# Three block products in place of four for the octonion gate and up projections of a two-layer model

## What is computed

```python
base = jnp.einsum('bsi,oi->bso', input, weight) + bias
labelers_A = lora_A[labeler_index]
ax = jnp.einsum('bsi,bir->bsr', input, labelers_A)
delta = jnp.einsum('bsr,or->bso', ax, lora_B)
return base + delta * LORA_SCALING
...
def ternary_dequant(W):
    scale = jnp.mean(jnp.abs(W))
    Wq = scale * jnp.clip(jnp.round(W / scale), -1.0, 1.0)
    return W + jax.lax.stop_gradient(Wq - W)
def oct_ternary_linear(xp, W):
    Wq = ternary_dequant(W)
    M = jnp.einsum('jik,jod->koid', S_OCT, Wq)
    return jnp.einsum('...id,koid->...ko', xp, M)
...
gate = oct_ternary_linear(xp, w_gate).reshape(B, T, -1)
up = oct_ternary_linear(xp, w_up).reshape(B, T, -1)
h = jax.nn.silu(gate) * up
out = oct_ternary_linear(hp, w_down).reshape(B, T, D)
```

## Time and profile before

| | us |
|---|---|
| median of 3 runs | 2195.96 |
| lowest and highest run | 2195.0 and 2197.66 |
| the profiled execution's own time | 2195.89 |
| its span, first to last instruction | 2194.0 |
| PE busy in the span | 2135.7 (97%) |
| DVE, ACT, POOL busy | 1277.6, 717.5, 1161.0 |
| mean granted TensorE clock, share of full | 0.991 |

### The profile page before, as it was taken

How to read it: one execution, slowest core, us unless ns; L and a number is a source line. 1 busy time by engine, 2 the same in 40 slices (tenths; PEclk the granted TensorE clock), 3 DMA queues, 4 the chain that set the end, 5 groups by cost and what they waited for, 6 DMA issues and landing times. The chain is left out here.

```text
span 2194.0 us, 36207 instructions
## 1 busy us (share of the span) xinstructions
PE 2135.7 (97%) x12004; PEld 1846.3 (84%) x12004; DVE 1277.6 (58%) x2346; ACT 717.5 (33%) x1474; POOL 1161.0 (53%) x1210
## 2 busy tenths in 40 slices
PE   7899999999999998999999999999979999999999
PEld 5688898989889897988989898898967788878887
DVE  7756566565656658565656657566557433334444
ACT  5333232332323323232323323233227533234332
POOL 3577676776857666675767767576720000014220
PEclk9999999999999998999999999999999999999999
DMA  7411220111121112111211111211113200001110
GB/s 234 147 49 39 58 58 30 47 38 38 38 67 48 39 39 77 39 39 40 62 43 48 38 38 38 67 48 39 50 41 122 86 0 0 0 0 36 41 39 19
DMA packets 92178, 110.71 MB, mean 50 GB/s; under 512 B 5536, under 2 KB 71744, under 8 KB 90960
## 3 DMA queue, kind: packets, MB, share of 16 engines
q1 hardware_dynamic: 90832, 105.67, 15.8%
q0 software_dynamic: 1280, 4.20, 0.6%
HBM read 103.93 MB, written 5.94 MB: 50 GB/s over the span
## 5 line engine op out<-in xcount | busy, mean ns | idle before, releaser
L171 PE MATMUL psum<-yc,wh 128*128 128x512 f32 x896 | 359.8, 402 | 10.2 <-DVE yc L1436 5.3
L172 PE MATMUL psum<-yc,wh 128*128 128x512 f32 x896 | 350.7, 391 | 0.0
L173 PE MATMUL psum<-yc,wh 128*128 128x512 f32 x896 | 350.4, 391 | 0.0
L1296 DVE TENSOR_TENSOR resid<-psum,resid 128x512 f32<-128x512 f32 x256 | 176.7, 691 | 158.4 <-PE psum L173 154.2
L171 PE MATMUL psum<-kept,yc 128*128 128x256 f32 x896 | 255.8, 286 | 1.7 <-DVE v_tok L1246 1.0
L173 PE MATMUL psum<-kept,yc 128*128 128x256 f32 x896 | 253.5, 283 | 0.0
L172 PE MATMUL psum<-kept,yc 128*128 128x256 f32 x896 | 253.4, 283 | 0.0
L896 POOL TENSOR_TENSOR wh<-wh_f,wh 128x256 fp32r<-128x256 f32 x256 | 191.3, 758 | 111.7 <-ACT wh L862 109.7
L2040 POOL TENSOR_TENSOR x_lo<-resid,x_hi 128x512 fp32r<-128x512 f32 x16 | 21.5, 1374 | 352.2 <-ACT x_hi L2076 352.2
L171 PEld LDWEIGHTS psum<-yc,wh 128*128 128x128 f32 x896 | 169.7, 189 | 43.2 <-DVE yc L1436 5.8
L173 PEld LDWEIGHTS psum<-yc,wh 128*128 128x128 f32 x896 | 169.0, 189 | 36.2
(11 more groups left out here) (299 smaller groups left out, 4748.3 us busy)
## 6 DMA issues: line engine op xcount, KB each, us to landing
raw<-in_attn_w SPq DMA_DIRECT2D x96, 512.0 KB, 4.9
wo_f<-in_attn_w SPq DMA_DIRECT2D x31, 512.0 KB, 4.0
hankel<-kernel_rows SPq DMA_DIRECT2D x32, 256.0 KB, 4.8
work_f<-in_oct_w SPq DMA_DIRECT2D x8, 680.0 KB, 4.0
resid<-in_xT SPq DMA_DIRECT2D x4, 1024.0 KB, 10.3
outT<-wide SPq DMA_DIRECT2D x16, 256.0 KB, 2.6
kept_f<-in_l_w SPq DMA_DIRECT2D x3, 1024.0 KB, 6.7
work_f<-in_oct_w SPq DMA_DIRECT2D x8, 384.0 KB, 3.2
```

The costliest lines, as they stand in the source:

```text
L171: pe.matmul(out, w[0], x[0], start=start, stop=False)
L172: pe.matmul(out, w[0], x[1], start=False, stop=False)
L173: return pe.matmul(out, w[1], x[0], start=False, stop=stop)
L1296: dve.tensor_tensor(part, psum[:, 5 + (GH + m) % 3, :], part, ALU.add).then_inc(tail_free, 1)
```

## The change

Hidden features are taken by component: the first 128 rows of each of the eight components, and the remaining 42 rows of each (8 x 42 = 336 rows in three slices of 126, 126 and 84). For a pair of components p and p+4 (`pair(p)`, four pairs) let A and B be the two blocks, and low and high the input halves (chunks 0, 1 and 2, 3). In place of A·low, B·high, B·low, A·high it computes three products for gate and three for up: a shared weight block times a sum of the halves, and two "cross" blocks (sum and difference of the two, with signs) times one half each. The two outputs are shared + first and shared + second. The sums come in six forms (`S_ARRAYS`: sum, difference, and two with mixed signs, of chunks 0+2 or 1+3), each split in hi and lo. The three slices of 42-row remainders are computed directly (`straight_product`). The down product is as before, over SLOTS = 11 slices in a new order of rows.

Matmuls per tile: 4 pairs x 2 matrices x 3 products x 2 chunks x 2 passes = 96, and 3 x 2 x 4 x 2 = 48, and 88 down.

```diff
-                    gate_up(0)
-                    gate_up(1)
-                    for h in range(2, HT):
-                        gate_up(h)
-                        down_product(h - 2)
-                    down_product(HT - 2)
-                    down_product(HT - 1)
...
+                    def shared(p, w):
+                        product(w, [main[:, 2 * c + w, 0, p * P:(p + 1) * P] for c in range(2)],
+                                [(s_hi[j], s_lo[j]) for j in PAIR_SUMS[p]])
+                    def crossed(p, w, form):
+                        product(1 + form, [main[:, 2 * c + w, form, p * P:(p + 1) * P] for c in range(2)],
+                                [z_chunk(c + (2 if form == 1 else 0)) for c in range(2)])
...
+                        shared(p, 0)
...
+                        shared(p, 1)
...
+                            pe.wait_ge(sum_done, before - 1)
+                        crossed(p, 0, 1)
...
+                        crossed(p, 0, 2)
+                        if p:
+                            down_product(2 * p - 2)
+                        pe.wait_ge(sum_done, before + 1)
+                        crossed(p, 1, 1)
+                        pe.wait_ge(sum_done, before + 2)
+                        crossed(p, 1, 2)
+                        if p:
+                            down_product(2 * p - 1)
...
+                    for d in range(3):
+                        straight_product(d)
+                        down_product(2 * PAIRS - 2 + d)
```

A shared product is copied from PSUM by ACT, and DVE adds each cross product to it:

```diff
+                    for p in range(PAIRS):
+                        for w, into in enumerate((gates, hid)):
+                            act.wait_ge(prod_done, tile * PRODUCTS + (6 * p + w + 1))
+                            act.activation(into[:, (2 * p + 1) % 4, :], psum[:, w, :], ACT.Copy).then_inc(copy_done, 1)
+                        for i in range(2):
+                            act.wait_ge(sum_done, tile * 4 * PAIRS + (4 * p + i + 1))
+                            silu(2 * p + i, gates[:, (2 * p + i) % 4, :])
...
+                    def add(p, w, i):
...
+                        dve.tensor_tensor(out[:, (2 * p + i) % 4, :], psum[:, 2 + i, :], out[:, (2 * p + 1) % 4, :],
+                                          ALU.add).then_inc(sum_done, 1)
...
+                        for i in range(2):
+                            dve.wait_ge(sum_done, tile * 4 * PAIRS + (4 * p + i + 3))
+                            times_gate(2 * p + i, hid[:, (2 * p + i) % 4, :])
```

POOL makes three of the six sums of the next tile and the lo part of all six; DVE makes the other three (`mixed_sum`), ACT the hi parts:

```diff
+                def next_sums(tile):
+                    for j, product in ((0, 2), (1, 8), (2, 8)):
+                        wait_apart(pool, prod_done, tile * PRODUCTS + product, passed)
+                        sum_of(tile + 1, j)
+                    for j in range(3):
+                        sums_low(tile + 1, j)
+                    for j in range(3, 6):
+                        sums_low(tile + 1, j)
```

```diff
+                ranks_high(NT - 1)
+                sign_main(NT - 1)
                 act.wait_ge(x_used, KC * (NT + 1))
-                for c in range(KC):
-                    first_z_high(c)
+                for c in (2, 3, 0, 1):
+                    z_high(0, c)
                 save_z(NT - 1)
-                sign_ternary(NT - 1, 2)
-                sign_ternary(NT - 1, 3)
+                for j in range(2, 6):
+                    sums_high(0, j)
...
+                straight_weights(3)
+                pool.wait_ge(comb_done, 8 * NT)
+                sum_of(0, 2)
+                for j in range(2, 6):
+                    sums_low(0, j)
+                for n in (8, 9, 10):
+                    sign_down_late(n)
```

More of the change, by code:

```diff
@@ L1671, in octonion_ffn @@
[L1671 to L1678, removed]
@@ new lines, in sign_down, with sums_high @@
+                def sign_down(n):
+                    _, k = down_piece(n)
+                    act.wait_ge(tern_step, tern_steps(n // 3, k))
+                    for i in range(OCT):
+                        at = slice(n * DIM + i * OD, n * DIM + (i + 1) * OD)
+                        r = down_rows(n)
+                        act.activation(down[0:r, at], down_raw[0:r, at], ACT.Copy, scale=signs(n, i)).then_inc(act_signed, 1)
+                def sums_high(tile, j):
+                    act.wait_ge((s_sum, s_mixed)[j // 3], tile * 3 + (j % 3 + 1))
+                    act.activation(s_hi[j], s_raw[j], ACT.Copy).then_inc(s_hi_done, 1)
@@ new lines, in hidden @@
+                    for p in range(PAIRS):
+                        for w in range(2):
+                            for i in range(2):
+                                add(p, w, i)
+                        for i in range(2):
+                            dve.wait_ge(sum_done, tile * 4 * PAIRS + (4 * p + i + 3))
+                            times_gate(2 * p + i, hid[:, (2 * p + i) % 4, :])
+                        for i in range(2):
+                            low(2 * p + i)
+                        if not last and p == 3:
+                            for j in (3, 4, 5):
+                                mixed_sum(tile + 1, j)
@@ new lines, in hidden @@
+                    for d in range(3):
+                        n, r = 2 * PAIRS + d, down_rows(2 * PAIRS + d)
+                        dve.wait_ge(prod_done, tile * PRODUCTS + (6 * PAIRS + 2 * d + 2))
+                        times_gate(n, psum[0:r, STRAIGHT_BANKS[d][1], :])
+                        if not last and d == 2:
+                            dve.wait_ge(s_sum, tile * 3 + 6)
+                            dve.wait_ge(s_mixed, tile * 3 + 6)
+                            z_low(tile + 1, 0)
+                        low(n)
@@ new lines, in product, with z_chunk @@
+                    def product(bank, weights, xs):
+                        for i, (wt, x) in enumerate(zip(weights, xs)):
+                            out = psum[0:wt.shape[1], bank, :]
+                            pe.matmul(out, wt, x[0], start=(i == 0), stop=False)
+                            mm = pe.matmul(out, wt, x[1], start=False, stop=(i == len(xs) - 1))
+                        mm.then_inc(prod_done, 1)
+                    def z_chunk(c):
+                        return z_hi[:, c, :], cols(z, c, tile)
```

471 lines of the change are left out of this document (330 added, 141 removed).

## The result

The changed kernel takes **2165.15 us** (median of four runs, 2162.63 to 2167.52), the kernel before 2196.81 beside it (2195.0 to 2197.82): a ratio of 0.9857, 95% interval 0.984 to 0.9874. The prediction said 2166, in 2161 to 2176. A second set of runs gave 2167.26 against 2196.03, 0.9872 (0.9855 to 0.9888). So the gain is 29 to 32 us. The total was right, but one term in it, the head of the feed-forward part, had the wrong sign, and others made up for it.

The account below looks back on a forecast made before the run. PE, busy 97% of the span, was taken as the bound. Terms -29.6 (128 matmuls) + 0.4 + 1.5 + 0.8 - 1.3 - 1.5 = -29.7 us from 2195.89 gave 2166 us, range 2161 to 2176.

Parts of the forecast that it names:

- the head of the feed-forward part: Entry of the first feed-forward tile, behind cond2: PE's stall and clock loss to be 3.9 against 5.2 us, -1.3.

Follow-up runs that it names:

- after: The profile of the changed kernel from its first set of runs, no further edit; median 2165.15 us.
- sum_first: Changed kernel with POOL making the first tile's third sum ahead of the last 16 narrow sign multiplications; 2165.82 us.
- pool_idle: Changed kernel without POOL's sums and low parts for tiles 1 to 3, POOL only passing signals on, output not the model's; 2164.25 us.
- late_sums: Changed kernel with POOL's three next-tile sums behind the 16th, 16th and 22nd product in place of the 2nd, 8th and 8th; 2162.48 us.
- no_table: Kernel of sum_first plus one single-column Silu on ACT ahead of the first tile's high parts; 2165.91 us.
- again: The changed kernel run once more without edits, as the measure for kernels beside it; 2167.26 us.
- pool_triple: Changed kernel with each of POOL's three next-tile sums made three times over in the same place; 2167.18 us.
- all_four: Changed kernel with four edits: third sum ahead of the signs, early Silu, later next-tile sums, last `save_z` split between ACT and DVE; 2158.91 us.
- shared_twice: Changed kernel with each shared product issued twice into the same bank, 128 matmuls more; 2189.79 us.

## What to carry to other kernels

Saved matmuls on an engine that is 97% busy were paid out at their start-to-start distance, nearly in full; most of the error was in the hand-overs and in the clock behind them. Work given to an engine "with room" has to be placed as well as counted: the same POOL instructions cost 1.2 us a tile or nothing, by where they stand against the neighbour's instructions with two SBUF operands. At a stage's head, walk the queue of every engine in order, with the contended durations, and ask of every waiting engine what its late work will meet next; removing 1.4 us of a wait there gave 0.3 us until, in the run with four edits, the collision behind it was moved too.

## What the runs showed of the hardware

- The clock doesn't follow from the length of one idle time. Behind 2.59 us without work at the entry of cond2, the granted clock fell in five profiles (after, sum_first, pool_idle, late_sums, no_table: 74.60 to 74.64 us) and not in four (again, pool_triple, all_four, shared_twice: 73.04 to 73.08). At the head a single wait of 2.96 us passed without a fall, while one of 2.17 (shared_twice) was followed by eight matmuls at 1.2 GHz.
- A wait costs more than its row shows. The waits listed with 0.8 us in cond2 cost 1.1 each, since the matmul behind the one that waited starts 0.1 us late too. The wait listed with 0.46 in the tiles costs 0.7, and 1.2 with the smaller one that follows it.
- POOL's multiplication of 42 columns took 0.39 us in all 14 cases with no instruction of DVE beside it, and up to 1.44 otherwise, median 0.55. What DVE does at the time says more about the price of so small an instruction than its columns.
- A meeting of POOL and DVE has no fixed price. Low part beside low part they slowed each other, 1.78 us on DVE and 1.64 to 1.72 on POOL. Beside three sums of POOL back to back (sum_first, 1732.4) one multiplication of DVE took 4.37 us, while the sums kept their 1.28 to 1.29.
- Each turn of the loop over tiles loaded ACT's table twice, 1.28 us each, before a Copy and before a Silu. One Silu ahead of the loop removed all of the loop's. Only the first of them was on PE's path: tile 2 is 54.47 us with and without.
